# Delta rule: token-indexed tiles on the other partition half, off-diagonal products of TensorE issued alternately with diagonal ones

## The chip, the core and the metric

The kernel runs on one core of a Trainium2 chip. The metric is the time on the device of one launch, in microseconds (us); lower is better. Only one stage of the kernel, the gated delta rule of layer 0, is touched by the change.

## The reference, cut to what matters

The whole computes two transformer-like layers on 4096 tokens of width 256. The stage of this case is the gated delta rule: 16 heads of size 64, a state of 64x64 for each head, one update a token.

```python
def step(S, inp):
    q_t, k_t, v_t, g_t, b_t = inp
    Sk = jnp.einsum('bhkv,bhk->bhv', S, k_t)
    delta = jnp.einsum('bhv,bhk->bhkv', v_t, k_t) - jnp.einsum('bhv,bhk->bhkv', Sk, k_t)
    S = jnp.exp(g_t)[..., None, None] * S + b_t[..., None, None] * delta
    o_t = jnp.einsum('bhkv,bhk->bhv', S, q_t)
    return (S, o_t)
...
o = _gated_delta_rule(q, k, v, g, beta).reshape(b, t, H * Kd)
return o @ Wo.T
```

## The kernel before, in words

The stage (`phase_delta`, from L690) does not walk token by token. It cuts the 4096 tokens into 64 chunks of 64 and takes two neighbouring chunks (x = 0 and 1) as a couple: 32 couples. Within a chunk the updates are coupled by a lower triangular 64x64 matrix for each head; its inverse is built by doubling blocks in five levels. Then the state passes through the chunk with a few dense products.

**Where data lies.** The 16 heads are 8 pairs p; head h of a pair has partitions 64h to 64h+63, in every tile. A "group" of TensorE work is the same product for all 16 heads: 16 calls of 64x64 by 64x64 in float32, written to one bank of PSUM [128, 8, 64]. Both operands of head h lie on partition half h and the result goes to half h, so every call uses one of the two quadrants on the diagonal of the array (rows half h, columns half h). The profile counts two matmuls and two weight loads for each float32 call, so a group is "x32" there.

**The groups of a couple**, 34 in all: keys_keys and keys_queries (one for each x), half and up (levels 1 to 5, one for each x), residual, updates, new_state (one for each x) and outputs (two products for each head, state by q and u by qk, so two groups for each x). Besides, `project` (L913) multiplies the outputs by Wo, 16 calls of 128 rows by 64 columns by 256, in two halves.

**Chains.** Inverse of one x at one level: TensorE half (upper by inv_low into pd_pre) -> VectorE mask_step (L1098) -> TensorE up (step by inv into pd_low) -> VectorE turn_low (L1106), and beside it ScalarE keep_inverse (L1012) -> next level. Head of it: keys_keys -> VectorE take_upper (L1059) -> GpSimd minus_eye (L1179) -> GpSimd first_inverse (L1184) -> VectorE turn_first (L1102) -> half. State: residual -> VectorE L1074 -> updates -> VectorE take_updates (L1087) -> outputs, and GpSimd decay_updates (L1188) -> new_state -> VectorE take_state (L1092) -> the residual of the next chunk.

**Order.** All is written out by hand, in program order for each engine, with counting semaphores. The loop over couples (`couples`, L792) calls `one(post, pre, ahead)` on every engine: the state work of couple post, the inverse of couple pre = post + 1, the loads and decays of couple ahead = pre + 1. There are 31 rounds with both post and pre, one with pre alone before and one with post alone behind them. On TensorE a round begins with keys_keys of pre and residual of post (L923 on). ScalarE's order has four blocks of copies across partitions a round (keep_rows L994, keep_values L1003, eight copies each) between the copies of the inverse. GpSimd's order in a round: decay_state, minus_eye 0, first_inverse 0, minus_eye 1, decay_updates 0, first_inverse 1, grow_queries, decay_state and decay_updates of x = 1, scatter, and for ahead decays, grow_keys, scale_rel (L1175).

SyncE loads for each couple k, q, v (512 KB each), rows, and four broadcasts of `sums` (running sums of the log decay, 128 KB each).

## Time and profile before

| | us |
|---|---|
| median of 3 runs (lowest to highest) | 4290.72 (4286.71 to 4294.25) |
| span of the profiled execution | 4287.6 |
| of it the delta stage, 540 to 1785 | 1245.0 |
| TensorE busy in the stage | 1196.75 |
| VectorE, ScalarE, GpSimd busy in the stage | 740.37, 731.74, 721.00 |

The profile has one line for each form of instruction, a timeline of instructions merged by form, a view of the busy time of each engine in chosen stretches (with the granted TensorE clock, 1.00 being full speed), and a view of who waited for whom. A timeline line gives start and length in us, engine, line, output<-inputs, shape, count, and in brackets the idle time before it and what ended it. PE is TensorE's matmul, PEld its weight load, DVE VectorE, ACT ScalarE, POOL GpSimd, SPq SyncE's queue. A length of a merged line reaches to the end of the last instruction, so the next line may begin before it is over.

### The profile page before, as it was taken

What the parts mean: (1) busy time and instruction counts of PE and PEld (TensorE: products, weight loads), DVE (VectorE), ACT (ScalarE), POOL (GpSimd) and SP (SyncE); (2) the same over time, 40 slices, a digit from 0 to 9 for tenths busy, and PEclk for the clock granted to TensorE, in tenths of its full rate; (3) what the DMA queues carried; (4) which work ended last, traced back from release to release, by engine and by line L of the source; (5) the groups of instructions that cost most, each with busy time, mean ns of one, the idle gap of its engine ahead of it and who ended that gap; (6) DMA issues with size and microseconds to landing.
All of it is one profiled execution on the core that took longest, in us unless ns stands there. A gap on an engine that the chain in (4) does not pass through costs nothing. (4 is left out here: it accounts for less than half of the span.)

```text
span 4287.6 us, 128339 instructions
## 1 busy us (share of the span) xinstructions
PE 4032.6 (94%) x52237; PEld 2492.3 (58%) x52237; DVE 3090.4 (72%) x5127; ACT 2445.9 (57%) x3901; POOL 1108.3 (26%) x1106
## 2 busy tenths in 40 slices
PE   5999789999999999997886999999999999999998
PEld 4444379999999999775663344444444444444443
DVE  5799855656665666444996787878878787878786
ACT  2788745656665556333442565656656565656554
POOL 1000065656656556202777000000000000000000
PEclk9999989999999999998997999999999999999999
DMA  3544422221212212224335000000000000000000
GB/s 125 177 127 128 138 95 71 74 71 62 73 65 74 74 63 70 65 90 143 107 109 124 8 5 19 5 8 15 10 15 10 13 5 20 5 20 3 10 15 10
DMA packets 261559, 248.47 MB, mean 58 GB/s; under 512 B 51712, under 2 KB 230016, under 8 KB 260256
## 3 DMA queue, kind: packets, MB, share of 16 engines
q1 hardware_dynamic: 240528, 209.29, 16.1%
q0 software_dynamic: 6144, 16.79, 1.2%
q10 hardware_dynamic: 14352, 14.55, 1.0%
q8 instruction: 423, 6.93, 0.7%
q14 instruction: 112, 0.92, 0.1%
HBM read 135.18 MB, written 105.38 MB: 56 GB/s over the span
## 5 line engine op out<-in xcount | busy, mean ns | idle before, releaser
L2245 DVE TENSOR_REDUCE part_max<-p_m 128x1 f32<-128x512 f32 x2118 | 1362.9, 685 | 379.8 <-PE p_m L2087 372.3
L2227 ACT ACTIVATE prob<-p_s 128x1024 f32<-128x1024 f32 x1024 | 1048.6, 1024 | 748.0 <-PE p_s L2151 746.1
L2106 PE MATMUL p_o<-prob,v_one 128*64 128x512 f32 x4096 | 1055.5, 592 | 3.9 <-ACT prob L2227 0.5
L2087 PE MATMUL p_m<-keys,queries 96*64 96x512 f16 x4236 | 662.0, 387 | 28.5 <-DMA keys<-parts_d 20.9
L2151 PE MATMUL p_s<-queries,keys 97*64 97x512 f16 x4096 | 619.6, 380 | 0.0
L2151 PEld LDWEIGHTS p_s<-queries,keys 97*64 97x64 f16 x4096 | 229.4, 109 | 597.7 <-issue 592.2
L2055 POOL TENSOR_TENSOR attn<-o_num,o_inv 32x512 f32<-32x512 f32 x64 | 81.0, 1266 | 1454.4 <-DVE o_inv L2264 1447.4
L2087 PEld LDWEIGHTS p_m<-keys,queries 96*64 96x64 f16 x4236 | 239.3, 108 | 309.7 <-DVE part_max L2245 56.3
L2106 PEld LDWEIGHTS p_o<-prob,v_one 128*64 128x64 f32 x4096 | 289.0, 136 | 162.5 <-issue 15.9
L858 PE MATMUL pd_pre<-inv_low,upper 64*64 64x64 f32 x10240 | 346.8, 219 | 14.1 <-DVE inv_low L1102 7.1
L588 PE MATMUL p_proj<-xn_t_all,proj_w_sb 128*128 128x512 f32 x768 | 337.9, 596 | 7.7 <-PEq L2390 7.7
L858 PEld LDWEIGHTS pd_pre<-inv_low,upper 64*64 64x64 f32 x10240 | 326.2, 135 | 29.4 <-issue 28.9
L858 PE MATMUL pd_low<-inv,step 64*64 64x64 f32 x10240 | 336.2, 219 | 1.0 <-DVE step L1098 0.7
L1098 DVE TENSOR_TENSOR step<-pd_pre,const 128x512 f32<-128x512 f32 x320 | 221.1, 691 | 150.8 <-PE pd_pre L858 150.7
L858 PEld LDWEIGHTS pd_low<-inv,step 64*64 64x64 f32 x10240 | 318.1, 135 | 18.3 <-issue 13.2
L1012 ACT ACTIVATE inv<-pd_low 128x512 f32<-128x512 f32 x256 | 152.9, 597 | 262.2 <-DVE inv_low L1106 261.2
L588 PEld LDWEIGHTS p_proj<-xn_t_all,proj_w_sb 128*128 128x128 f32 x768 | 146.9, 191 | 193.0 <-issue 187.8
L1106 DVE STREAM_TRANSPOSE inv_low<-pd_low 128x512 f32<-128x512 f32 x256 | 183.6, 717 | 74.3 <-PE pd_low L858 74.3
L1003 ACT ACTIVATE v_row<-v_turned 32x256 f32<-32x256 f32 x512 | 212.1, 414 | 6.7
L994 ACT ACTIVATE k_row<-k_turned 32x256 f32<-32x256 f32 x512 | 211.5, 413 | 6.0
L1059 DVE TENSOR_TENSOR upper<-pd_pre,upper 128x512 f32<-128x512 f32 x64 | 44.3, 692 | 151.9 <-PE pd_pre L858 134.8
L905 PE MATMUL pd_a<-q_t,state 64*64 64x64 f32 x2048 | 128.5, 221 | 10.5 <-DVE u L1087 10.4
(235 smaller groups left out, 5843.7 us busy)
## 6 DMA issues: line engine op xcount, KB each, us to landing
q_d<-conv_q SPq DMA_DIRECT2D x16, 1024.0 KB, 5.0
v_d<-conv_v SPq DMA_DIRECT2D x16, 1024.0 KB, 5.0
k_d<-conv_k SPq DMA_DIRECT2D x16, 1024.0 KB, 6.5
sums<-sums_d SPq DMA_DIRECT2D x128, 128.0 KB, 3.0
k_t<-k_d SPq DMA_DIRECT2D x32, 512.0 KB, 4.8
q_t<-q_d SPq DMA_DIRECT2D x32, 512.0 KB, 3.4
v_t<-v_d SPq DMA_DIRECT2D x32, 512.0 KB, 5.5
slots_d<-zero ACTq DMA_DIRECT2D x1, 10112.0 KB, 32.6
```

Source lines behind the costliest of these rows:

```text
L588: last = te.matmul(p_proj[u % RING][:], g.proj_w_sb[:, n, c, p * P:(p + 1) * P], g.xn_t[:, c, b * BLK:(b + 1) * BLK], start=c == 0, stop=c ...
L858: last = te.matmul(out[hs, p, :], lhs(p, hs), rhs(p, hs), start=True, stop=True)
L994: last = a.activation(k_row[to_p, x, :, to_t], k_turned[x][from_p, :, from_t], ACT.Copy)
L1003: last = a.activation(v_row[to_p, x, :, to_t], v_turned[x][from_p, :, from_t], ACT.Copy)
L1012: a.activation(inv[x][:] if k < NL else inv_fin[:, n.ring[x]], p_low[x][:], ACT.Copy).then_inc(up_d[x], 1)
L1098: v.tensor_tensor(step[x][:], p_pre[x][:], over_pairs(masks[:, k - 1, :]), ALU.mult).then_inc(step_d[x], 1)
L1106: v.transpose(inv_low[x][:], p_low[x][:]).then_inc(lowc_d[x], 1)
L2087: last = te.matmul(p_m[k % 2][x * HALF:(x + 1) * HALF, :], queries[0:ROW, p, hh, at:at + HALF], keys[0:ROW, 2 * p + hh, kb * BLK:(kb + 1) ...
L2106: product = te.matmul(p_o[64 * hh:64 * hh + VW, :], g.v_one[:, j, p, hh:hh + 2, :].rearrange("p a d -> p (a d)"), prob[:, j % 2, hh, :], s ...
L2151: last = te.matmul(p_s[j % 2][x * HALF:(x + 1) * HALF, hh, :], keys[0:KR, 2 * p + hh, at:at + HALF], queries[0:KR, p, hh, :], start=True, ...
L2227: a.activation(prob[:, j % 2], p_s[j % 2][:], ACT.Exp, scale=SCORE_SCALE).then_inc(exp_d, 1)
L2245: v.tensor_reduce(part_max[:, hh * SUB + sub, kb:kb + 1], p_m[k % 2][:], AX.X, ALU.max).then_inc(red_d, 1)
```

## The change

1. Everything indexed by token (gates beta and cum, k_row and v_row, resid, u, u_dec, qk, upper, inv, step) of head h moves to partition half 1-h; k, q, k_g, grow, the state and the outputs stay on half h. The host swaps the two heads of each pair in the gate weights, `blocks_of` writes the turned blocks to the other half, and `sums_k` is a second copy of the sums for `grow` (9 key loads a couple for 5).
2. So ten groups a couple cross from one half to the other and use the off-diagonal quadrants: keys_keys, keys_queries, residual, the u by qk part of outputs, new_state. The other 24 stay on the diagonal.
3. TensorE's program is written anew: groups are zipped, one call of the one, one call of the other, for each head. In a full round nine such pairs stand: old_outputs + residual of x = 0; updates 0 + keys_queries 1; half 0 level 1 + new_outputs 0; half 1 level 1 + new_state 0; up 1 level 1 + residual 1; half 0 level 3 + new_outputs 1; up 0 level 3 + new_state 1; and, at the end, up 0 and up 1 of level 5 with keys_keys 0 and 1 of the couple ahead. Both results of a pair are signalled at its end.
4. outputs is cut in old_outputs (state by q, beside the residual) and new_outputs; PSUM pd_a and pd_b become four banks pd_r, pd_o, pd_u, pd_n.
5. The tile diff goes; decays and exponential work in place in rel, and related's three waits move from ScalarE to GpSimd's decays. VectorE's order and one ScalarE copy (keep_outputs of x = 1, from level 2 to 3) are moved.

The diff, cut to its core:

```diff
-    KEY_LOADS = 5
+    KEY_LOADS = 9
...
-    p_a, p_b = ps("pd_a"), ps("pd_b")
+    p_r, p_o, p_u, p_n = ps("pd_r"), ps("pd_o"), ps("pd_u"), ps("pd_n")
...
+        to = (1 - h) * C
         for a in range(2):
             for b in range(2):
                 yield (slice(h * C + b * B32, h * C + (b + 1) * B32), slice(a * B32, (a + 1) * B32),
-                       slice(h * C + a * B32, h * C + (a + 1) * B32), slice(b * B32, (b + 1) * B32))
+                       slice(to + a * B32, to + (a + 1) * B32), slice(b * B32, (b + 1) * B32))
 
...
-                    sp.dma_start(sums[h * C:(h + 1) * C, x].rearrange("p n t -> p (n t)"),
-                                 spread(g.sums_d[bass.ds(n.chunk[x], 1), h, :], [C, NPAIR * C])).then_inc(k_in[n.odd], 16)
+                    for dst, half in ((sums, h), (sums_k, 1 - h)):
+                        sp.dma_start(dst[half * C:(half + 1) * C, x].rearrange("p n t -> p (n t)"),
+                                     spread(g.sums_d[bass.ds(n.chunk[x], 1), h, :], [C, NPAIR * C])).then_inc(k_in[n.odd], 16)
...
+        def rows_of(half):
+            return slice(half * C, (half + 1) * C)
+        def product(p, h, out, to, lhs, rhs, start=True, stop=True, shared=False):
+            return te.matmul(out[rows_of(h if to == SAME else 1 - h), p, :], lhs(p, rows_of(h)), rhs(p, rows_of(h)), start=start, stop=stop,
+                             skip_group_check=shared)
...
+        def old_outputs(n, x, p, h):
+            return product(p, h, p_o, SAME, of(state), of_couple(q_t, n.ring[x]), start=p == 0, stop=False, shared=True)
...
+        def wait_outputs(n, x):
+            wait_each(pe, (att_d[x], n.now), (u_d, n.ended[x]))
+        def new_outputs(n, x, p, h):
+            return product(p, h, p_o, OTHER, of(u), of(qk, n.ring[x]), start=False, stop=p == NPAIR - 1, shared=True)
...
+        def over_heads(*products):
+            for p in range(NPAIR):
+                for h in range(2):
+                    last = [one_product(p, h) for one_product in products]
+            return last
...
+        def first_part(post, pre):
+            if post is not None:
+                wait_state(post, 0)
+                _, last = over_heads(lambda p, h: old_outputs(post, 0, p, h), lambda p, h: residual(post, 0, p, h))
+                last.then_inc(res_d, 1)
+            if pre is not None:
+                wait_queries(pre, 0)
+                over_heads(lambda p, h: keys_queries(pre, 0, p, h))[0].then_inc(qk_d[0], 1)
+                wait_queries(pre, 1)
+            if post is not None:
+                wait_updates(post, 0)
+            if post is not None and pre is not None:
+                new, asked = over_heads(lambda p, h: updates(post, 0, p, h), lambda p, h: keys_queries(pre, 1, p, h))
+                new.then_inc(w_d, 1)
+                asked.then_inc(qk_d[1], 1)
+                wait_half(pre, 0, 1)
+                wait_outputs(post, 0)
+                low, out = over_heads(lambda p, h: half(pre, 0, p, h), lambda p, h: new_outputs(post, 0, p, h))
+                low.then_inc(half_d[0], 1)
+                out.then_inc(o_d, 1)
+                wait_half(pre, 1, 1)
+                wait_new(post, 0)
+                low, new = over_heads(lambda p, h: half(pre, 1, p, h), lambda p, h: new_state(post, 0, p, h))
+                low.then_inc(half_d[1], 1)
+                new.then_inc(new_d, 1)
...
+        def both_parts(post, pre, ahead):
+            wait_up(pre, 0, 1)
+            over_heads(lambda p, h: up(pre, 0, p, h))[0].then_inc(upmm_d[0], 1)
+            wait_up(pre, 1, 1)
+            wait_state(post, 1)
+            grown_up, res = over_heads(lambda p, h: up(pre, 1, p, h), lambda p, h: residual(post, 1, p, h))
+            grown_up.then_inc(upmm_d[1], 1)
+            res.then_inc(res_d, 1)
+            over_heads(lambda p, h: old_outputs(post, 1, p, h))
+            halves(pre, 2)
+            wait_updates(post, 1)
+            over_heads(lambda p, h: updates(post, 1, p, h))[0].then_inc(w_d, 1)
+            ups(pre, 2)
+            wait_half(pre, 0, 3)
+            wait_outputs(post, 1)
+            low, out = over_heads(lambda p, h: half(pre, 0, p, h), lambda p, h: new_outputs(post, 1, p, h))
+            low.then_inc(half_d[0], 1)
+            out.then_inc(o_d, 1)
+            wait_half(pre, 1, 3)
+            over_heads(lambda p, h: half(pre, 1, p, h))[0].then_inc(half_d[1], 1)
+            wait_up(pre, 0, 3)
+            wait_new(post, 1)
+            grown_up, new = over_heads(lambda p, h: up(pre, 0, p, h), lambda p, h: new_state(post, 1, p, h))
+            grown_up.then_inc(upmm_d[0], 1)
+            new.then_inc(new_d, 1)
+            wait_up(pre, 1, 3)
+            over_heads(lambda p, h: up(pre, 1, p, h))[0].then_inc(upmm_d[1], 1)
+            halves(pre, 4)
+            project(post, range(0, NPAIR // 2))
+            ups(pre, 4)
+            halves(pre, 5)
+            project(post, range(NPAIR // 2, NPAIR))
...
+            for x in range(2):
                 if pre is not None:
-                    up(pre, 0, k)
-                    up(pre, 1, k)
-                if post is not None and k <= 3:
-                    (updates, outputs, new_state)[k - 1](post, 1)
-                if post is not None and k == 4:
-                    project(post, range(0, NPAIR // 2))
-                if pre is not None:
-                    half(pre, 0, k + 1)
-                    half(pre, 1, k + 1)
-            if post is not None:
-                project(post, range(NPAIR // 2, NPAIR))
-            if pre is not None:
-                up(pre, 0, NL)
-                up(pre, 1, NL)
+                    wait_up(pre, x, NL)
+                if ahead is not None:
+                    wait_keys(ahead, x)
+                if pre is not None and ahead is not None:
+                    grown_up, keyed = over_heads(lambda p, h: up(pre, x, p, h), lambda p, h: keys_keys(ahead, x, p, h))
+                    grown_up.then_inc(upmm_d[x], 1)
+                    keyed.then_inc(kk_d[x], 1)
...
+            gaps = rel[:, n.ring[x], :, 1:]
+            a.activation(gaps, gaps, ACT.Exp).then_inc(rel_d[x], 1)
...
                 take_upper(pre, 0)
+                take_upper(pre, 1)
             if post is not None:
                 residual(post, 0)
             if pre is not None:
-                take_upper(pre, 1)
                 attention(pre, 0)
                 turn_first(pre, 0)
             if post is not None:
                 take_updates(post, 0)
             if pre is not None:
                 attention(pre, 1)
-                turn_values(pre, 0)
                 turn_first(pre, 1)
                 mask_step(pre, 0, 1)
             if post is not None:
                 take_state(post, 0)
             if pre is not None:
                 mask_step(pre, 1, 1)
-            if post is not None:
-                residual(post, 1)
+                turn_values(pre, 0)
             for k in range(1, NL):
                 if pre is not None:
                     turn_low(pre, 0, k)
+                if post is not None and k == 1:
+                    residual(post, 1)
+                if post is not None and k == 3:
+                    take_state(post, 1)
+                if pre is not None:
                     turn_low(pre, 1, k)
-                if post is not None and k in (1, 3):
-                    (take_updates if k == 1 else take_state)(post, 1)
                 if pre is not None and k == 2:
                     turn_keys(pre, 0)
                     turn_values(pre, 1)
@@ -1141,6 +1248,8 @@
                 if pre is not None:
                     mask_step(pre, 0, k + 1)
                     mask_step(pre, 1, k + 1)
+                if post is not None and k == 1:
+                    take_updates(post, 1)
 
...
+            gaps = rel[:, n.ring[x], :, 1:]
+            if not n.first:
+                pool.wait_ge(att_d[x], n.before)
+                pool.wait_ge(relb_d[x], n.before)
+                pool.wait_ge(udec_d, n.older[x])
             pool.wait_ge(k_in[n.odd], n.key_loads)
-            po.tensor_tensor(diff[x][:], sums[:, x], per_pair(g.cum, n.chunk[x]), ALU.subtract).then_inc(diff_d[x], 1)
+            po.tensor_tensor(gaps, sums[:, x], per_pair(g.cum, n.chunk[x]), ALU.subtract).then_inc(diff_d[x], 1)
             pool.wait_ge(diff_d[x], n.now)
-            po.tensor_tensor(diff[x][:], diff[x][:], over_pairs(g.c("future")), ALU.add).then_inc(min_d[x], 1)
+            po.tensor_tensor(gaps, gaps, over_pairs(g.c("future")), ALU.add).then_inc(min_d[x], 1)
 
...
+    wg = a["L0_attn_Wg"].reshape(NPAIR, 2, D)[:, ::-1]
+    wb = a["L0_attn_Wb"].reshape(NPAIR, 2, D)[:, ::-1]
...
```

`halves(n, k)` and `ups(n, k)` issue the groups of both x at level k one after the other, unpaired; SAME and OTHER name the half that a result goes to.

## Rows read from the trace of the kernel before

**Rows 1.** Busy time by stretch: stage, then about one couple (busy us, count).

```profile
core 0: us, PE busy (x) PEld busy (x) DVE busy (x) ACT busy (x) POOL busy (x), PEclk, DMA share, GB/s
540.00:1785.00 1245.00, 1196.75 (x35832) 1122.50 (x35834) 740.37 (x1088) 731.74 (x1567) 721.00 (x672) 0.99 0.21 68
1000.00:1037.20 37.20, 36.80 (x1113) 34.67 (x1108) 23.14 (x34) 22.54 (x49) 21.86 (x21) 1.00 0.21 69
```

**Rows 2.** Timeline, ScalarE: one copy for each couple, two rounds in a row.

```profile
999.67 0.39 ACT L1028 ACTIVATE attn_tok<-pd_b 128x256 f32<-128x256 f32 x1 [4.37 <-PE pd_b L919]
...
1037.57 0.39 ACT L1028 ACTIVATE attn_tok<-pd_b 128x256 f32<-128x256 f32 x1 [4.37 <-PE pd_b L919]
```

**Rows 3.** Timeline, TensorE, same round: groups back to back, project, first passes.

```profile
1001.47 1.10 PE L858 MATMUL pd_pre<-k_t 64*64 64x64 f32 x32
1002.40 1.10 PE L858 MATMUL pd_a<-state,k_g 64*64 64x64 f32 x32
...
1031.69 1.95 PE L919 MATMUL pd_b<-wo,o_t 128*64 128x256 f32 x16
1033.56 0.27 PE L858 MATMUL pd_pre<-inv_low,upper 64*64 64x64 f32 x2
```

**Rows 4.** Timeline, VectorE and GpSimd, same round: head of the inverse's chain.

```profile
1002.62 0.69 DVE L1059 TENSOR_TENSOR upper<-pd_pre,upper 128x512 f32<-128x512 f32 x1 [4.13 <-PE pd_pre L858]
...
1003.39 1.27 POOL L1179 TENSOR_TENSOR upper<-upper,const 128x512 f32<-128x512 f32 x1 [3.42 <-DVE upper L1059]
1004.80 1.28 POOL L1184 TENSOR_TENSOR inv<-upper,const 128x512 f32<-128x512 f32 x1
1006.04 1.27 POOL L1179 TENSOR_TENSOR upper<-upper,const 128x512 f32<-128x512 f32 x1
1007.49 1.06 POOL L1188 TENSOR_TENSOR u_dec<-u,rel 128x512 f32<-128x512 f32 x1 [0.17 <-DVE u L1087]
1008.50 1.27 POOL L1184 TENSOR_TENSOR inv<-upper,const 128x512 f32<-128x512 f32 x1
...
1009.81 0.71 DVE L1102 STREAM_TRANSPOSE inv_low<-inv 128x512 f32<-128x512 f32 x1 [1.12 <-POOL inv L1184]
...
1011.30 1.15 PE L858 MATMUL pd_pre<-inv_low,upper 64*64 64x64 f32 x32
```

**Rows 5.** Timeline, same round: from a VectorE result to TensorE, and ScalarE's copies.

```profile
1017.38 0.69 DVE L1098 TENSOR_TENSOR step<-pd_pre,const 128x512 f32<-128x512 f32 x1 [0.17 <-PE pd_pre L858]
...
1018.23 0.22 PE L858 MATMUL pd_low<-inv,step 64*64 64x64 f32 x1
...
1016.94 3.39 ACT L1003 ACTIVATE v_row<-v_turned 32x256 f32<-32x256 f32 x8
```

**Rows 6.** Timeline, attention stage; and the page's group of full-width float32 matmuls.

```profile
3001.20 1.04 PE L2106 MATMUL p_o<-prob,v_one 128*64 128x512 f32 x4
3002.06 0.61 PE L2151 MATMUL p_s<-queries,keys 97*64 97x512 f16 x4
...
L588 PE MATMUL p_proj<-xn_t_all,proj_w_sb 128*128 128x512 f32 x768 | 337.9, 596 | 7.7 <-PEq L2390 7.7
```

**Rows 7.** L128 (wait_each), 1012.3 to 1013: two waits of TensorE's queue.

```profile
L128 PEldq EVENT_SEMAPHORE  x2: 51/51/51, 1012.4 to 1012.8; - x2
```

**Rows 8.** Timeline, TensorE: idle spells and the work behind them.

```profile
1765.35 1.15 PE L858 MATMUL pd_b<-resid,inv_fin 64*64 64x64 f32 x32 [0.95 <-DVE resid L1074]
...
1771.73 1.15 PE L858 MATMUL pd_a<-state,k_g 64*64 64x64 f32 x32 [1.25 <-ACT o_t L1017]
1773.82 1.93 PE L858 MATMUL pd_b<-resid,inv_fin 64*64 64x64 f32 x32 [0.94 <-DVE resid L1074]
...
2059.39 0.68 PE L1703 MATMUL ps_sum<-v_ones,k_feat 128*128 128x129 f32 x4 [1.96 <-DVE k_feat L1839]
```

**Rows 9.** Busy time by stretch around those spells; the clock is the third number from the end.

```profile
2047.00:2060.00 13.00, 10.73 (x75) 9.14 (x75) 12.07 (x32) 6.45 (x18) 9.91 (x15) 1.00 0.39 100
2060.00:2064.00 4.00, 4.00 (x12) 2.35 (x11) 3.50 (x10) 1.74 (x6) 3.41 (x5) 0.58 0.49 146
1756.00:1774.00 18.00, 13.91 (x357) 11.85 (x355) 5.18 (x8) 11.89 (x28) 2.12 (x2) 1.00 0.01 3
1774.00:1785.00 11.00, 9.16 (x152) 8.41 (x151) 1.38 (x2) 1.62 (x4) 3.17 (x4) 0.69 0.07 25
```

156 lines of the change are left out of this document (83 added, 73 removed).

## The prediction, made before the changed kernel ran

> **What bounds the kernel now.** I read the stretches first: the stage takes 1245.0 us of the span and TensorE (PE) is busy for 1196.75 of them, while the three other engines are busy for 720 to 740 [rows 1]. So the stage hangs on PE. Two copies that occur once a couple stand 37.90 us apart [rows 2]; 31 full rounds at that pace are 1175 us, the rest is the first and the last round. Then the timeline inside one round: a group starts 0.93 us behind the one before, and project's half takes 1.87 [rows 3]. 34 groups and two halves: 34 x 0.93 + 3.74 = 35.4 us. So PE idles or starts up for 2.5 us a round, and only fewer or shorter PE slots can give much.
>
> **What the pairs save on PE.** A group has 32 passes in 0.93 us, 29 ns for one. Do the two diagonal quadrants already work side by side? A full-width float32 pass of 512 columns costs 337.9 / 768 = 0.44 us [rows 6], so one of 64 columns would be 0.055 us; 0.029 is half. They do. The four passes of p_o in the attention stage begin at 3001.20 and the next work at 3002.06 [rows 6]: 0.86 us for four passes of 512 columns, which alone are 0.44 each. These are two column halves that share all rows of the array, so sharing a row half costs nothing either. What no row shows is two row halves writing the same PSUM partitions at once, in two banks. That is the only new thing in a pair of a diagonal and an off-diagonal group. Bounds: a pair costs as little as one group, 0.93 us, or as much as two, 1.87 us (beyond that only if the quadrants hindered one another, for which no row speaks). I take 0.95, since three of the four neighbourhoods of quadrants are seen at full rate. Can the queue feed it? A pair has 128 instructions. Between the waits at 1012.4 and 1012.8 lie the 64 instructions of a residual [rows 7], so at most about 0.5 us for 64 and 1.0 for 128: just enough. There are nine pairs a round (keys_queries 0 stands alone), so PE's own work falls to 35.4 - 9 x 0.91 = 27.2 us.
>
> The Trainium skill speaks against this: its page "TensorE: Matmul & The Clock Gate", section "Part 3: Packing small matmuls", says that a weight load overlaps matmuls in flight only if the row group differs; by it the pairs would gain nothing, as in the rival "two wide" below. In rows 6 the two column halves share the row group and still overlap. The page "TensorEngine Tiling (Array Packing)", section "Restrictions and Gotchas", allows different row tiles at once if they write different PSUM banks, as the pairs do; no run here shows that yet.
>
> **What the round becomes.** With 27.2 us of PE work the chains bind in part, so I walk through a round, T = 0 where old_outputs + residual begin. Links: a group's start to the VectorE (DVE) operation that reads it 1.15 us (1001.47 to 1002.62) [rows 3, 4]; DVE start to PE start 0.85 (1017.38 to 1018.23) [rows 5]; DVE operations back to back about 0.65.
>
> Head of the inverse: from keys_keys 0 to half of x = 1 it is 1011.30 - 1001.47 = 9.83 us now, of which GpSimd and DVE alone need 9.2 (1.15 + 0.77 + 1.41 + 1.24 + 1.45 + 1.01 + 1.31 + 0.87, step by step) [rows 3, 4]. keys_keys 0 now begins at T = -1.9, so half 1 + new_state 0 can't begin before T = 7.3. Until then PE has: keys_queries 0 from 0.95; updates 0 + keys_queries 1 from 2.02 (residual's result 1.17, DVE 0.85) to 2.97; half 0 + new_outputs 0 from 4.16 (u waits for updates at 3.2 and for turn_first ahead of it on DVE) to 5.11. PE idles 1.2 and 2.2 us.
>
> From there: pair 7.30; up 0 8.25; up 1 + residual 1 at 9.93 (mask_step 1 stands behind take_state 0 on DVE: 8.47, 9.08, and 0.85); old_outputs 10.88; half 0, 1 of level 2 11.81, 12.74; updates 1 13.67; up 14.6, 15.5; half 0 level 3 + new_outputs 1 16.63; half 1 17.58; up 0 level 3 + new_state 1 19.35 (DVE has two transposes ahead of the mask); up 1 20.3; half level 4 21.4, 22.7; project 23.95 (its o_t copy was moved behind the level 3 copies on ScalarE, which end at 23.2, and takes 0.6); up level 4 25.85, 26.8; half level 5 27.9, 28.8; project 29.8; up level 5 + keys_keys 31.75, 32.7; end 33.65. Some eight starts from idle cost a little more (the first passes last 0.27 rather than 0.22 us [rows 3, 5]): 0.5 a round with rounding up. So 34.15 us for 37.90.
>
> **The other edits.** The sums' four more broadcasts are 0.5 MB a round on DMA engines busy for 0.21 [rows 1]: hidden, the keys being needed only at T = 31.7; at the stage's start, where nothing hides them, 2 us. SyncE's other loads stand behind them, with as much slack. ScalarE has four copy blocks of 3.39 us [rows 5]; its copy of level 1 of x = 1 comes at 12.5, keep_values follows to 16.5, and the level 2 copies are there at 18.05, before 19.35: hidden by 1.3 us. related's three waits on GpSimd are for work finished by T = 17; decays start at 19.4 and grow_keys end at 26.4: nothing. Copies to the other partition half are the same eight of 32 partitions: nothing (bounds: they cross quadrants already). The last round has half the outputs beside other work: 2 us less. Start and end cancel.
>
> **The clock.** Granted 1.00 in the full rounds, where PE is busy for 36.80 of 37.20 us [rows 1]. After 1.96 us of idleness the clock falls: 1.00, then 0.58 over 4 us [rows 8, 9], which is 3.4 us at 1.2 GHz, (1 - 0.58) / 0.5 x 4. After 1.25 and 0.94 us with one group between, the next group takes 1.93 for 1.15 us [rows 8], and 0.69 is granted from there [rows 9]. The changed round has 1.2 and 2.2 us of idleness with one pair between: nearer to those rows than to a full round of today. A fall costs: 3.4 us at half speed, some 0.6 in the idle spell, the other 2.8 does half its work, so 1.4 us. I take it in five rounds of six: 1.2 us a round (bounds 0 and 1.7).
>
> **The sum.** 37.90 - 34.15 - 1.2 = 2.55 us a round, x 31 = 79 us. The profiled span is 4287.6, the median 3.1 above it. 4287.6 - 79 = 4208.6 by the profile, 4212 by the median.
>
> **Rivals.** *Four wide, the clock holds:* 3.75 x 31 = 116 less, 4175. For it: pairs use all four quadrants, and an idle spell of 0.95 us at 1765 left the clock at 1.00 until 1774 [rows 8, 9]. Against: the other rows 8.
>
> *Two wide (the slower side).* If row halves can't write the same partitions at once, a pair is 1.87 us and PE's work is about what it is now, while both results of a pair come at its end. Then up 1 + residual 1 ends at 14.4 rather than 10.9 (3.5 later), and the four later pairs add 0.93 each: 33.65 + 3.5 + 3.7 - 0.7 absorbed in waits = 40.2 us a round, 2.3 more than now: 71 more, 4362. The clock holds. What speaks for it is only that no row shows the thing. Between a pair of 0.95 (34.15 us) and of 1.87 (40.2) I draw a line: the round is 37.9 again where a pair costs 1.52 us, and from there on the change loses.
>
> *Partly wide,* a pair at 1.25 us because weight loads or PSUM writes meet: by that line 36.1 us a round, the clock hardly falling: 1.7 x 31 = 53 less, 4238.
>
> *Fed too slowly,* instructions coming no faster than one pass in 25 ns, a pair of 64 passes at 1.6 us: by the line 38.4 us, 4307, just slower. Against it: 32 passes with their loads entered the queue in under 0.5 us [rows 7], under 16 ns a pass. The same page of the Trainium skill ("TensorE: Matmul & The Clock Gate", section "Back-to-back issue gap") puts such a floor of about 25 ns on matmuls however few their columns.
>
> **How the numbers follow.** Four wide with clock falls 0.42 (4212), four wide without 0.25 (4175), partly wide 0.15 (4238), two wide 0.14 (4362), fed too slowly 0.04 (4307). The likeliest is 4212. Range: the first three, with half a microsecond a round either way (15 us) and the upper end drawn out for a pair at 1.4 us: 4135 to 4285; the two slower cases are left out. A measurement tells about 0.2% (8.6 us) from no change: faster 0.80 (a little of partly wide goes off), within 0.04 (a pair near 1.52), slower 0.16.
>
> **What would show it.** A pair's 64 passes within about 0.95 us; copies of attn_tok 34 to 35.5 us apart; PE's busy share of a round near 0.8, with idle spells before half 1 + new_state 0 released by inv_low; clock under 1.00 in the full rounds, in spells right after these. Wrong if the pair takes 1.87 us, or if PE waits for a ScalarE copy or a DMA anywhere.

## The result: 0.4% slower, and the profile after

| | before | after |
|---|---|---|
| median, us (lowest to highest) | 4288.72 (4286.23 to 4294.25) | 4308.85 (4300.98 to 4311.72) |
| ratio, 95% interval | | 1.004 (1.0028 to 1.0053) |
| span of the profiled execution, us | 4287.6 | 4306.8 |

The forecast was 4212 and the range ended at 4285: the change loses 20 us where 79 were to be gained. Busy time by stretch in the kernel after (columns as in [rows 1]; the third number from the end is the granted clock):

```profile
540.00:1785.00 1245.00, 1027.63 (x35552) 936.25 (x35552) 709.90 (x1083) 721.68 (x1544) 709.14 (x666) 0.92 0.25 81
1000.00:1037.20 37.20, 29.98 (x1105) 27.50 (x1103) 21.55 (x33) 22.17 (x48) 20.03 (x20) 0.95 0.24 82
1017.00:1021.00 4.00, 3.88 (x126) 3.89 (x127) 2.45 (x4) 2.78 (x7) 2.52 (x3) 0.58 0.01 4
1021.00:1031.60 10.60, 9.33 (x360) 8.94 (x358) 7.27 (x12) 7.12 (x16) 2.94 (x4) 1.00 0.02 5
```

TensorE is busy for 29.98 of 37.20 us, against 36.80 in [rows 1]: the busy time fell as the pairs should make it, and every other engine does less work in the same stretch, so no other engine took TensorE's place as the bound. The time went into gaps of TensorE. Its timeline in the round from 1006 on, the lines with an idle spell of over 1 us ahead of them, and the VectorE line behind the first:

```profile
1011.28 0.21 PE L863 MATMUL pd_r<-state,k_g 64*64 64x64 f32 x1 [2.10 <-issue]
...
1014.72 0.24 PE L863 MATMUL pd_pre<-inv_low,upper 64*64 64x64 f32 x1 [1.13 <-DVE u L1193]
...
1017.12 0.27 PE L863 MATMUL pd_pre<-inv_low,upper 64*64 64x64 f32 x1 [1.71 <-issue]
...
1025.66 1.32 PE L863 MATMUL pd_pre<-inv_low,upper 64*64 64x64 f32 x37 [1.11 <-issue]
```
```profile
1011.60 0.69 DVE L1180 TENSOR_TENSOR resid<-v_row,pd_r 128x512 f32<-128x512 f32 x1 [2.58 <-PE pd_r L863]
```

Only the second is an idle spell that the walk foresaw, the one before half 0 + new_outputs 0. The others were foreseen by nothing. Ahead of the first, three pairs had run one behind the other (up 0 and up 1 with keys_keys, old_outputs + residual), and then the last pass of residual, behind no wait, came 2.1 us late. "issue" says that TensorE waited for nothing that the profile shows. VectorE's first step of the state, and all that hangs on it, stood behind that one pass. The third stands in the middle of half 0 + new_outputs 0: 58 of its 128 instructions had run, and the next, which waits for no semaphore, came 1.7 us late. The fourth stands in the same way inside half 0 of level 2. The second foreseen spell, before half 1 + new_state 0, is not there in this round; by the records a wait stands there in 21 of 30 rounds, 0.94 us a round on average. The page's group of half shows that it is no single case (103.1 us idle ahead of it, 56.5 put down to issue):

```profile
L863 PE MATMUL pd_pre<-inv_low,upper 64*64 64x64 f32 x10240 | 397.3, 234 | 103.1 <-issue 56.5
```

**A tally for all kernels.** I went through the records of 30 full rounds of each kernel, from one copy to attn_tok to the next. A gap is a distance of over 110 ns between the starts of two successive TensorE instructions, less the usual 55; it is "inside groups" where the later instruction waits for no semaphore, "waits" where it does. "Low clock" is the time at a granted 1.2 GHz. All in us a round; the columns overlap where an idle spell falls into the low clock. Distances between two passes of project, and of the fillers below, are not counted as gaps. The waits are the roughest column: counting the semaphore instructions in another way moves them by up to 0.6 us.

```
chip                    round  gaps inside groups  waits  low clock
1  before               38.05   0.84               0.79   0.00
1  after                38.72   4.95               3.07   5.80
2  before_again         39.23   1.79               0.82   0.11
2  after_again          40.51   5.72               2.89   7.85
2  lean                 50.68   3.86               4.24  11.04
2  before_project8      39.10   1.66               0.79   0.00
3  unzipped             39.99   3.10               2.11   0.80
3  filler               40.34   5.51               2.42   3.07
3  spread               40.00   5.35               2.68   7.28
4  after_third          40.49   5.58               2.73   8.99
4  unzipped_again       40.05   3.16               2.11   0.68
4  hybrid               40.77   4.65               2.86   6.83
5  half_before          35.56   0.00               1.60   0.00
5  half_unzip           34.27   0.00               5.66   0.00
5  half_zip             33.59   1.00               6.06   2.84
5  half_zip_filler      32.91   0.02               4.16   0.00
```

(The 1.00 of half_zip is no stop: its passes are long enough at the low clock to count as a gap.) "Chip" tells the sets of runs apart; only within a set are times compared. After's round closes roughly from the prediction's own terms: 27.2 of work (the forecast's figure, not a measured one), 3.07 of waits (foreseen 3.4), and 4.95 of gaps inside groups (foreseen 0). To that comes the half speed of 5.80 us: 2.9 if all of it fell on work, 2.3 without the 1.2 us of it that fall into waits and gaps (foreseen 1.2). That makes 37.5 to 38.1 of 38.72. The theory for the experiments: TensorE's instructions arrive too slowly for two products at once. The stage is written out without branches (`couples` is a Python loop), so a jump can't be what holds the instructions up.

### The profile page after: what moved, and what is told of

It reads as the page before. It is cut to its first block and busy times, and to the rows that moved or that the text cites. A ratio compares the mean times of both kernels' runs of the same rounds, so it can differ in the third digit from the quotient of the medians.

```text
span 4306.8 us, 128467 instructions
## 1 busy us (share of the span) xinstructions
PE 3878.8 (90%) x52237; PEld 2318.4 (54%) x52237; DVE 3062.9 (71%) x5127; ACT 2444.4 (57%) x3901; POOL 1101.5 (26%) x1106
## 5 line engine op out<-in xcount | busy, mean ns | idle before, releaser
L863 PE MATMUL pd_pre<-inv_low,upper 64*64 64x64 f32 x10240 | 397.3, 234 | 103.1 <-issue 56.5
L863 PEld LDWEIGHTS pd_pre<-inv_low,upper 64*64 64x64 f32 x10240 | 364.3, 147 | 120.7 <-issue 115.5
L863 PE MATMUL pd_low<-inv,step 64*64 64x64 f32 x10240 | 373.2, 229 | 26.8 <-issue 24.9
L863 PEld LDWEIGHTS pd_low<-inv,step 64*64 64x64 f32 x10240 | 349.0, 144 | 59.6 <-issue 57.7
L1301 POOL TENSOR_TENSOR u_dec<-u,rel 128x512 f32<-128x512 f32 x64 | 67.7, 1058 | 290.8 <-DVE u L1193 290.8
L2377 DVE RECIPROCAL o_inv<-o_raw 128x64 f32<-128x64 f32 x256 | 137.8, 541 | 0.0
```

Of the source, the lines that this page charges most:

```text
L863: return te.matmul(out[rows_of(h if to == SAME else 1 - h), p, :], lhs(p, rows_of(h)), rhs(p, rows_of(h)), start=start, stop=stop, skip_gr ...
```

## The experiments

The theory (SUPPLY) against three rivals: the new order or its waits cost it (ORDER), the clock does (CLOCK), or single places in the round do (PLACE).

### Unzipped: the new order, products one behind the other

```diff
         def over_heads(*products):
-            for p in range(NPAIR):
-                for h in range(2):
-                    last = [one_product(p, h) for one_product in products]
+            last = []
+            for one_product in products:
+                for p in range(NPAIR):
+                    for h in range(2):
+                        done = one_product(p, h)
+                last.append(done)
             return last
```

> The changed kernel with the same order of groups and the same waits, but the two groups of each pair one after the other instead of call by call, each signalled at its own end. The quadrants then work two at a time. Theory A (the zipped pairs do run four quadrants at once, and what is gained is lost again to instruction fetch and to the clock): nine pairs cost 0.93 us each more of TensorE work, 8.4 us a round; the stops behind an instruction fetch fall from 2.4 us a round to the 0.5 of the kernel before, the time at the low clock from 5.9 us a round to about 0. Sum: 38.7 + 8.4 - 1.9 - 1.7 less what the idle spells of 4 to 5 us absorb, 39 to 41 us a round, 4320 to 4380 us. Theory B (pairing saves nothing that counts; the new order is what made it slower): within 5 us of the changed kernel's 4309.

Measured: 1.0066 (1.0049 to 1.0083), 4348.78 against 4317.28. That is inside the time range of Theory A, but not by its sum: the gaps did not fall to what the kernel before has, and nine pairs did not cost 8.4 us. So most of the loss stands without the interleaving: gaps inside groups are 3.10 us a round, between before's and after's. The timeline tells why they are there at all. Three of its lines, where up 0 goes over into keys_keys 0:

```profile
1025.15 0.97 PE L863 MATMUL pd_low<-inv,step 64*64 64x64 f32 x26
1025.91 0.27 PE L863 MATMUL pd_pre<-k_t 64*64 64x64 f32 x2
1025.96 0.28 PE L863 MATMUL pd_low<-inv,step 64*64 64x64 f32 x3
```

The product issued second starts before the last passes of the first, and they alternate from there: the engine itself runs a following product on the free quadrants beside the one ahead. Written in turn, the six groups at the round's end still overlap in part, and so also ask for instructions faster than before. The clock is hardly low here (0.80 us a round), so the loss of this kernel is not one of the clock alone.

### Burst: the price of a pair by itself

At the stage's start, with nothing to wait for, 8 times two groups in turn, 12 pairs, and 4 times two groups in turn (k_t by k_t, same half and other half):

```diff
+        wait_keys(first, 0)
+        for _ in range(8):
+            over_heads(along)
+            over_heads(aside)
+        for _ in range(12):
+            over_heads(along, aside)
+        for _ in range(4):
+            over_heads(along)
+            over_heads(aside)
```

> The changed kernel with extra products at the start of the delta stage, into two banks that are free then: 8 diagonal and 8 off-diagonal groups in turn, unzipped; then 12 zipped pairs without any wait between; then 4 and 4 unzipped. Theory A (TensorE's instructions arrive in blocks of 256, at best one block in 3.3 us): the unzipped groups take 0.93 us each; of the 12 zipped pairs the first two or three take 0.93 to 0.95 each, then there are stops, each ending some 1.2 us behind the end of an instruction DMA, and the average falls to 3.3 / 2 = 1.65 us a pair, 17 to 20 us for 12. Rival (the stops come of a wait, a bank or a port): 12 pairs in 12 x 0.94 = 11.3 us without a stop. The kernel is longer by the added work, some 40 us.

Timeline of TensorE (first pass behind a stop), busy time by stretch, and the DMA queues from 572.7 to 586.79 (packets, MB, share of 16 engines):

```profile
569.25 0.27 PE L863 MATMUL pd_u<-k_t 64*64 64x64 f32 x1 [1.64 <-issue]
...
572.70 0.27 PE L863 MATMUL pd_u<-k_t 64*64 64x64 f32 x1 [1.36 <-issue]
```
```profile
569.25:586.79 17.54, 11.03 (x640) 10.34 (x640) 0.00 (x0) 0.00 (x0) 0.00 (x0) 1.00 0.02 5
572.70:574.58 1.88, 1.88 (x128) 1.88 (x128) 0.00 (x0) 0.00 (x0) 0.00 (x0) 1.00 0.03 9
576.16:578.04 1.88, 1.88 (x128) 1.88 (x128) 0.00 (x0) 0.00 (x0) 0.00 (x0) 1.00 0.03 9
```
```profile
q8 instruction: 4, 0.07, 1.8%
```

The kernel took 4393.38 us (one run), and the 12 pairs 20.6 us, for 17 to 20 expected by Theory A and 11.3 by its rival. Two things stand in these lines. First, 128 matmuls and 128 weight loads, two whole pairs, run in 1.88 us at a clock of 1.00: **a pair costs 0.94 us**, as I had taken it. Second, then everything stops, and the next 128 begin 3.45 us behind the last ones (569.25, 572.70, 576.16), over and over, though no instruction waits for anything. Each time one packet of 16 KB comes in on the queue named "instruction": 4 packets in 14.1 us. By this trace 16 KB are 256 instructions: just so many run between two stops. So supply is **256 instructions in 3.45 us, 13.5 ns each**; where a packet took longer, the distance was 3.73 us (565.52 to 569.25, and 583.06 to 586.79). The packet itself fills only some 0.95 of the 3.45 us. It begins 1.0 to 1.2 us behind the first instruction of the block that is running, and the new block's first instruction runs 1.3 to 1.4 us behind the packet's end. So three delays stand one behind the other, and the bandwidth is not the limit. A pair eats 128 in 0.94 us, 7.3 each; one group 64 in 0.93, 14.6 each. The kernel before, 256 in 3.73 us, ran 8% inside the faster figure and right at the slower one; a pair needs nearly twice of it. That is SUPPLY shown by itself; ORDER, CLOCK and PLACE have no part in this stretch.

The trace of after agrees in detail: the late pass at 1011.28 comes 1.2 us after the end of an instruction packet (1009.11 to 1010.04), the one at 1017.12 1.6 us after that of the next (1014.62 to 1015.55). In 30 rounds there are 66 stops of over 1 us that wait for no semaphore, each ending 1.2 to 1.6 us behind a packet's end (0.9 to 1.7 in the ten other runs named below), and counted in TensorE's instructions all 65 distances between them are whole multiples of 256. So are all 270 such distances in ten other runs with groups of 16 calls (before, unzipped, filler, spread, hybrid, before_project8 and the four repeats). In the full rounds of no kernel do two fetches begin under 3.2 us apart.

That is a limit of short stretches, not of the average: a round of after has 2265 instructions in TensorE's queue, semaphore waits included, 8.8 blocks. At 3.45 us each they would take 30.5 us of 38.72 (an estimate from burst's distance). So the stops come where pairs bunch the demand; that supply left unused while the engine idles or runs project is lost, and not stored up, is the likely reading. The Trainium skill, page "Runtime: NRT & Kernel Launch", section "Instruction fetch mechanics", describes this fetch in blocks of 256 instructions and calls its cost mostly hidden. The block is as the trace has it; hidden it is not, with stops of 1.6 us in burst.

### Filler and spread: more clock, and a lighter turn of the round

Filler puts one full-width product of no use before half 0 + new_outputs 0 and two before half 1 + new_state 0, into the idle spells ahead of the low clock. Spread moves a quarter of project in between the two up + keys_keys pairs, so that no three pairs stand in a row.

```diff
+        def filler(times):
+            for _ in range(times):
+                te.matmul(p_n[:].rearrange("p n t -> p (n t)"), wo[:, 0, 0:P], wo[:, 0:2, :].rearrange("p n d -> p (n d)"), start=True, stop=True)
...
+                filler(1)
                 wait_half(pre, 0, 1)
...
+                filler(2)
                 wait_half(pre, 1, 1)
...
-            project(post, range(NPAIR // 2, NPAIR))
+            project(post, range(NPAIR // 2, 3 * NPAIR // 4))
...
+                if x == 0 and post is not None and pre is not None:
+                    project(post, range(3 * NPAIR // 4, NPAIR))
```

> The changed kernel with three extra matmuls of 128x128 by 128x512 a round in TensorE's two idle spells (one ahead of half 0 + new_outputs 0, two ahead of half 1 + new_state 0), 0.86 us each, 12 instructions in all, into pd_n, which is overwritten afterwards. Theory (the clock falls because of these spells): the time at the low clock goes from 5.9 us a round to under 1, and of the 5.9 some 3.4 lie on work, half of which is lost: 1.7 us a round, 53 us, 4256 us. Rival (the low clock falls into idle time and costs nothing): 4305 to 4325, the clock at 1.00 all the same. If the fillers stand in the way of the chain they cost up to 0.5 us a round, 15 us.

> The changed kernel with project's second half split: a quarter ahead of up 0 + keys_keys 0, a quarter between it and up 1 + keys_keys 1 (64 instructions in 1.87 us, four times fewer per us than in a pair). Theory A (256 instructions used up in under 3.3 us stop TensorE): the stop of about 2 us behind the three pairs at the end of the round shrinks by 1 us or more, and the chain through keys_keys 0 starts 0.9 us earlier: 1.5 to 2.3 us a round less, 4238 to 4262 us. Rival (fetch is not the cause): only the 0.9 us of the chain, 4281 us.

Measured: filler 1.0109 (1.0091 to 1.0127), spread 1.0057 (1.004 to 1.0074). Filler took the low clock from 7.85 us a round (after, on another chip) to 3.07, and no gain shows: the 4256 us that were expected of 4309 did not come. That a faster array only meets the next stop sooner is the likely reason, and not shown: where the second spell is missing (9 of 30 rounds in after), the fillers are added work. CLOCK falls as the cause of the whole loss, by this and by unzipped, which loses with hardly any low clock; the clock's price at this count of instructions stays open. Spread was forecast at 4238 to 4262 us of 4290 and missed it. Its 1.0057 lies between after's 1.004 on the first chip and 1.009 and 1.0078 on two others, and after did not run beside it, so no gain is shown; gaps inside groups stayed at 5.35 us. Its timeline shows small ones among them, as here on either side of eight instructions:

```profile
1002.54 0.25 PE L863 MATMUL pd_o<-qk,u 64*64 64x64 f32 x1 [0.40 <-issue]
...
1003.28 0.25 PE L863 MATMUL pd_o<-qk,u 64*64 64x64 f32 x1 [0.41 <-issue]
```

### The same again beside two kernels with fewer instructions

after_again and before_again are the two kernels unchanged. Lean replaces the unpaired half and up products by 8 calls of 128x128 by 64 for 16 of 64x64, and before_project8 is the kernel before with project's 16 calls made 8 of 128 columns:

```diff
+                last = te.matmul(out[:, p, :], g.c("eye"), rhs[:, p, :], start=True, stop=True)
...
-                    last = te.matmul(out[x * C:(x + 1) * C, 0:D], o_t[:, x, p, :], wo[:, p, :], start=p == 0, stop=p == NPAIR - 1)
+                last = te.matmul(out[:, 0:D], o_t[:, p].rearrange("p x t -> p (x t)"), wo[:, p, :], start=p == 0, stop=p == NPAIR - 1)
```

> The changed kernel once more, unedited, so that what follows has it on its own chip. Expected 1.004 of the kernel before; TensorE idle inside groups, with nothing to wait for, for about 5 us a round, at the low clock 5.8 us a round.

> The kernel before once more, unedited, for its trace on this chip. Expected: idle inside groups 0.8 us a round, never at the low clock.

> The changed kernel with 13 of its unpaired groups (all half and up groups that stand alone) issued as 8 calls of 128x128 by 64 with a constant identity as stationary operand, instead of 16 calls of 64x64 by 64: the same columns streamed for nearly the same time (8 x 2 x 2 x 53 ns halved by nothing: 0.85 to 0.93 us), half the instructions. The computation of the inverse is left out by it. Instructions a round fall from 2272 to 1856, blocks fetched from 8.9 to 7.3. Theory A (instruction supply bounds the round): 1.6 blocks of 3.4 us less to fetch, idle time inside groups from 5 to about 1.5 us, less about 0.8 us of switching between tile shapes: 35 to 36.5 us a round for 38.7, 0.98 to 0.985 of the kernel before, 4200 to 4235 us where that is 4290. Rival (the chains and the clock bound it; fetch stops fall into time that is idle anyway): not below 38 us a round, 1.00 to 1.005.

> The kernel before with project as 8 calls of 128x128 by 256 instead of 16 of 128x64 by 256 (both chunks of the couple in one stationary operand; o_t laid out for it): 32 instructions a round fewer and 16 slots of 0.213 us for 17.3: 0.2 to 0.4 us a round by TensorE's own time, 6 to 12 us, 0.997 to 0.9985 of the kernel before. Rival (a weight load of 128 columns is not hidden behind 256 columns, or project stands beside a wait): no change.

Measured: after_again 1.009 (1.0073 to 1.0107), for 1.004 expected; before_again 4323.41 beside 4322.03; lean 1.104 (1.0961 to 1.112), its runs from 4725.51 to 4820.54; before_project8 0.9998 (0.9989 to 1.0008). The change loses on each chip, but not the same: 0.4% on the first, 0.8 and 0.9% on two others. The kernel before differs too, 0.84 and 1.79 us of gaps inside groups a round, where 0.8 was expected again. What is added are small gaps: those of 0.5 to 1 us, mostly 8 to 13 instructions apart, are 1.26 us a round in before_again for 0.42 in before, and 2.06 in after_again for 0.61 in after, while stops of over 1 us are fewer there (3.17 us a round for 3.98). Why is open. Before_project8 has 32 instructions fewer of 2240 in a round (matmuls and weight loads) and gains nothing that can be measured, where 0.15 to 0.3% was expected.

Lean is no test of the theory. Its products of 128 columns of weights take about twice one group, and the round is 50.7 us. A pass takes 112 ns for the same 64 columns streamed, where one quadrant of before takes a pass in 58 (29 ns a pass, two quadrants at once). What was widened is the block of weights, from 64x64 to 128x128; that loading it is what binds is the likely reading, and was not tested by itself. It took away instructions and put in a slower thing, so it says nothing of SUPPLY.

### Half the instructions for the same columns

The test that lean should have been: each call streams the 128 columns of two neighbouring pairs of heads against a constant block of 64x64, so that banks, columns, waits and order stay and calls are halved. Half_before is that edit of the kernel before, half_unzip and half_zip of the new order without and with interleaving, half_zip_filler adds the filler.

```diff
-            for p in range(NPAIR):
+            for p in range(0, NPAIR, 2):
...
-            return te.matmul(out[rows_of(h if to == SAME else 1 - h), p, :], lhs(p, rows_of(h)), rhs(p, rows_of(h)), start=start, stop=stop,
+            return te.matmul(out[rows_of(h if to == SAME else 1 - h), p:p + 2, :], g.c("eye")[rows_of(h), rows_of(h)], rhs(p, rows_of(h)), start=start,
```

> The changed kernel with half the calls in the same way: 1152 TensorE instructions a round for 2240, 4.5 blocks for 8.9, a pair 64 instructions in 0.9 us. Theory A (the pairs' gain is eaten by the supply of instructions): idle time inside groups from 5.7 us a round to under 0.7, and the round from 40.5 to what was predicted, 34 to 36 us; 0.96 to 0.975 of the kernel before. Rival B (waits and clock eat it): idle time inside groups falls too but waits grow as much; 38 us a round or more, 0.99 or more.

> The kernel half_zip with its pairs unzipped: one group behind the other. Theory A (with enough instructions four quadrants are worth what was predicted): 2.5 to 4.5 us a round slower than half_zip, 37 to 39.5 us. Rival B (pairing is worth nothing, as between the changed kernel and its unzipped form): within 1 us a round of half_zip.

> half_zip with the three 128x512 fillers of the run filler in TensorE's idle spells. Theory (with supply out of the way the price of the clock shows): low clock from 6 to 10 us a round to under 2, the round 1 to 2 us shorter than half_zip. Rival (the fillers cost as much as the clock gives back): within 0.5 us, or longer.

> The kernel before with half the calls: each 64x64 call of a group streams 128 columns (two pairs of heads) against one stationary operand, a 64x64 block of a constant identity. The same columns, banks, quadrants, waits and nearly the same TensorE time (a group: 32 passes of 64 columns become 16 of 128), but 32 instructions a group for 64. The stationary operands, and so the products, are left out by it. Theory A (supply of instructions costs 1.8 us a round here in the kernel before, and a start-up cost falls with each call saved): 36 to 37.5 us a round for 39.2, 0.985 to 0.99 of the kernel before. Rival (supply costs nothing): 38.3 or more.

| | median, us | ratio to the kernel before (95%) | round, us |
|---|---|---|---|
| half_before | 4205.27 | 0.9802 (0.9786 to 0.9819) | 35.56 |
| half_unzip | 4169.0 | 0.9716 (0.97 to 0.9732) | 34.27 |
| half_zip | 4149.54 | 0.9669 (0.9653 to 0.9685) | 33.59 |
| half_zip_filler | 4128.72 | 0.9624 (0.9608 to 0.964) | 32.91 |

The page's line of the instruction queue in half_zip, then in after:

```profile
q8 instruction: 288, 4.72, 0.5%
```
```profile
q8 instruction: 424, 6.95, 0.7%
```

Busy time by stretch, half_zip, then half_zip_filler:

```profile
600.00:1600.00 1000.00, 865.88 (x17140) 751.34 (x17142) 659.74 (x1011) 680.30 (x1458) 668.08 (x627) 0.96 0.29 91
```
```profile
600.00:1600.00 1000.00, 936.85 (x17650) 761.20 (x17645) 672.81 (x1030) 689.23 (x1475) 670.90 (x631) 1.00 0.29 91
```

With 136 blocks fewer the stops are gone, and the change comes near to what the walk said: 33.59 us a round for a walked 34.15, though with calls that are themselves shorter by the column (a group takes 0.87 us for 0.93). And now both idle spells stand where the walk put them, with the releaser that the prediction named for the second:

```profile
1020.01 0.29 PE L863 MATMUL pd_pre<-inv_low,const 64*64 64x128 f32 x1 [1.22 <-DVE u L1193]
...
1023.08 0.44 PE L863 MATMUL pd_pre<-inv_low,const 64*64 64x128 f32 x1 [1.96 <-DVE inv_low L1208]
```

Each part now has a price of its own: the new order 1.3 us a round (35.56 to 34.27), the interleaving 0.7 (to 33.59), the clock 0.7 (to 32.91; granted 0.96, then 1.00). The filler that was useless at full count is worth 21 us here. ORDER falls: fed well, the new order, with its products on all four quadrants, is the largest gain, not a loss. The expectations missed in part: half_before came out faster than foreseen (35.56 for 36 to 37.5), half_unzip far faster (34.27 for 37 to 39.5), so that "within 1 us a round of half_zip", its rival, holds by the number; and the filler gave 0.7 us where 1 to 2 were expected. Of half_before's 2.5 us (35.56 for 38.05 in before) only 0.84 can be gaps inside groups; the rest is mostly the shorter group, and halving the calls also halves the weight loads. So the ladder shows the stops going with the instructions, but not the price of supply by itself; that is burst's.

Why is the interleaving worth so little? Six groups of half_unzip at the round's turn, first and last line:

```profile
1022.12 0.76 PE L863 MATMUL pd_low<-inv,const 64*64 64x128 f32 x10
...
1025.54 1.04 PE L863 MATMUL pd_low<-q_t,const 64*64 64x128 f32 x16
```

The second line follows the six, so they took 3.42 us, 1.14 for two. One group of half_before takes 0.87, two in turn 1.75. So the engine finds two thirds of the overlap by itself once neighbouring groups lie on different quadrants; writing them call by call adds the rest, and part of that goes into waits.

### How much is the interleaving, and does it sit in one place?

The changed kernel and unzipped side by side in five rounds, and hybrid: only the three pairs at the round's turn issued one product behind the other, all others interleaved.

```diff
+        def in_turn(*products):
+            return [over_heads(one_product)[0] for one_product in products]
...
-                _, last = over_heads(lambda p, h: old_outputs(post, 0, p, h), lambda p, h: residual(post, 0, p, h))
+                last, _ = in_turn(lambda p, h: residual(post, 0, p, h), lambda p, h: old_outputs(post, 0, p, h))
...
-                    grown_up, keyed = over_heads(lambda p, h: up(pre, x, p, h), lambda p, h: keys_keys(ahead, x, p, h))
+                    keyed, grown_up = in_turn(lambda p, h: keys_keys(ahead, x, p, h), lambda p, h: up(pre, x, p, h))
```

> The changed kernel, unedited, beside its unzipped form on one chip. Expected 1.004 to 1.009 of the kernel before.

> The unzipped form of the changed kernel once more, on the same chip. Theory A (with all its instructions the round is bounded by their supply, and the 8.4 us that pairing saves on TensorE are given back): within 1 us a round, 0.7%, of the changed kernel, and not slower by more than 0.3%. Rival (pairing is worth something, and the two calls before, on which the comparison rests, were too unlike): 1 us a round slower or more.

> The changed kernel with only the three pairs at the turn of the round unzipped (keys_keys first, then up of level 5, for both x; then residual 0 and old_outputs 0): 384 instructions that took 2.8 us take 5.6, slower than they are supplied, and keys_keys 0 ends 0.9 us sooner before what follows. The six pairs that follow a wait stay zipped. Theory A: the stop of some 2 us at the turn goes, the added TensorE time is 2.8 us: 0.3 to 1.2 us a round less than the changed kernel by the earlier keys_keys and the absent low clock, 0.995 to 1.002 of the kernel before. Rival: the added 2.8 us count in full, 1 us a round more than the changed kernel.

Measured: after_third 1.0078 (1.0064 to 1.0092), unzipped_again 1.0054 (1.004 to 1.0068), hybrid 1.009 (1.0076 to 1.0103). Interleaving costs about 0.24% at full count (the intervals overlap by a hair, but the slowest run of unzipped_again, 4348.89, is below the fastest of after_third, 4350.79). Across chips the comparison says nothing: unzipped's 1.0066 lies between after's 1.004 and 1.009. PLACE falls as well: hybrid is no better (0.995 to 1.002 was expected), with 4.65 us of gaps still inside groups. Since stops stand at whole blocks of 256 and a round has 2265 instructions, they fall on other groups in each round, and moving the demand moves the stop.

## Why the prediction was wrong, by its own steps

**Pairs at 0.95 us: right, when the instructions are there.** 0.94 in burst. Two row halves write the same partitions in two banks at full rate, which no row of before showed. The rule of the Trainium skill weighed there ("TensorE: Matmul & The Clock Gate", section "Part 3: Packing small matmuls") would have given 1.87 for one pair; two pairs ran in 1.88 us. Nor does the floor of about 25 ns that its section "Back-to-back issue gap" states bind here: the passes of burst are 14.7 ns apart (1.88 us by 128).

**"Can the queue feed it? ... just enough": the step that failed.** The 64 instructions that enter within 0.5 us in [rows 7] were there already. One group says nothing of what comes behind it; the supply has to be read over more instructions than are stored. The kernel before held the hint: 256 instructions in 3.73 us wherever groups stand back to back [rows 3], and a queue of instruction packets on the page that I did not set against that:

```profile
q8 instruction: 423, 6.93, 0.7%
```

What the runs showed in its place is a supply of 256 instructions in 3.45 us at best, where nine pairs ask for 256 in 1.9. The term is 4.95 us a round where I had nothing, less the 0.84 that before has too: 4.1 us, 127 us in 31 rounds. It is enough by itself to turn the forecast gain of 79 into a loss, and more than the 99 us that the forecast missed by: a stop also takes the place of waits and idleness that I had counted, as with the second spell.

**The walked round (34.15): near where it is fed**, 33.59 with the clock falling, 32.91 without. The walk had no clock in it, so 32.91 is its counterpart. It is 1.2 us less; 25 slots of 0.87 for 0.93 us would be up to 1.5 (an estimate), so some of the nearness may be luck. The real products were not measured with a full supply. In half_zip the two idle spells are 1.22 and 1.96 us for a walked 1.2 and 2.2. In after the first is there; the second is partly taken up by stops.

**The clock: mechanism right, size wrong at full count.** Granted 0.58 from 1017 to 1021, just behind three idle spells of 2.10, 1.13 and 1.71 us, two of which are stops; in [rows 9] it fell behind idleness too. But the stops add idleness of their own: 5.80 us a round at 1.2 GHz, 2.3 to 2.9 lost by halves, where I had 1.2. When fed, the fall is worth 0.7, under my 1.2. What it is worth at full count no run tells: filler removed most of it and no gain showed.

**The other edits: next to nothing, and right.** The view of waits names no load and no GpSimd operation ahead of TensorE in the rounds of after. ScalarE's copy of o_t does hold up project, in half_zip 31 times by at most 0.2 us: 5.5 us in all, against the prediction's last line.

**Rivals.** "Fed too slowly" gave 4307 and the measured median is 4308.85. It is the right rival, at 0.04, but its mechanism was another: not 25 ns a pass in a steady flow, but 27 ns a pass (13.5 an instruction) on average, in blocks at full rate with stops between. That it meets the number within 2 us is partly luck, since it left out the clock. It was dismissed by the same reading of [rows 7]. "Two wide" is excluded by burst. Its walk is not tested by half_unzip, whose groups still overlap by half and more.

**What stays open.** Why before's gaps inside groups differ between chips by 0.95 us a round; what a round with the real products takes when it is fully fed; how many instructions are stored, and whether another order of the same calls could avoid the stops; whether before's group, 0.93 for half_before's 0.87, is held up by supply (14.6 ns an instruction against 13.5) or by its weight loads; and why, with the store empty, instructions also come in eights, 0.6 to 0.7 us apart, as in spread, on the later chips and hardly on the first.

## What to carry to other kernels

Before you pack small products, count instructions over a stretch of a few microseconds and set them against the instruction packets on the page: here 256 in 3.45 us was the ceiling in a steady burst, and back-to-back groups at 256 in 3.73 had 8% to gain from packing, not half. The packing that pays makes each instruction bigger, as the halved calls do (up to 3.8% below the kernel before, though they leave out the real products), and, as far as lean shows, it must not widen the weight load beyond the columns streamed. An engine that is busy for 96% of a stage can still hide a second limit right behind it.

## What the runs showed of the hardware that I had not expected

- TensorE's instructions come in 16 KB blocks of 256, in burst one in 3.45 to 3.73 us; it runs them at 7.3 ns each when they are there, then stands for 1.6 us, and resumes 1.3 to 1.4 us after the packet's end (1.2 to 1.6 in after).
- All stops of over 1 us behind no semaphore, in the rounds of after and of ten other runs, stand whole multiples of 256 instructions apart.
- Products on different quadrants overlap though issued one behind the other: two groups in 1.14 us for 1.75.
- Quadrants that share a row half, and row halves that write the same partitions in two banks, all work at full rate: four at once.
- 64 columns against a 128x128 block of float32 weights take 112 ns a pass (lean), against 64x64 blocks on two quadrants 29 (before).
